# Output bias of the attention stages: one-row matmuls on TensorE, or an addition on GpSimd

## The reference

```python
# L1: cross-attention with padding mask, 16 heads
xn = layer_norm(x, g_x, b_x); kvn = layer_norm(kv, g_kv, b_kv)
... softmax(q k^T * scale) v ...
return out @ w_proj + b_proj
# L2: cross-attention, 16 heads, biases on q, k, v
return ctx @ Wo + bo
# L2 feed-forward part: first a causal self-attention without any bias
x = x + attention(layernorm(x, ln1_w), c_attn_w, c_proj_w)   # y @ c_proj_w
# L3: cross-attention, 8 heads of 64
return out @ Wout + bout
x = x + <the above>
```

## Time and profile before

| | us |
|---|---|
| median of 3 runs (lowest to highest) | 3641.53 (3633.49 to 3645.52) |
| the profiled execution, its own time | 3635.24 |
| its span, first to last instruction | 3633.5 |
| TensorE matmuls busy in the span | 2925.8 (81%) |
| VectorE busy | 2018.9 (56%) |
| ScalarE busy | 1661.6 (46%) |
| GpSimd busy | 813.2 (22%) |

### The profile page before, as it was taken

How to read it: one execution, slowest core, us unless ns; L and a number is a source line. 1 busy time by engine, 2 the same in 40 slices (tenths; PEclk the granted TensorE clock), 3 DMA queues, 4 the chain that set the end, 5 groups by cost and what they waited for, 6 DMA issues and landing times. The chain is left out here.

```text
span 3633.5 us, 71573 instructions
## 1 busy us (share of the span) xinstructions
PE 2925.8 (81%) x26488; PEld 1935.1 (53%) x26488; DVE 2018.9 (56%) x4658; ACT 1661.6 (46%) x3102; POOL 813.2 (22%) x772
## 2 busy tenths in 40 slices
PE   4888676888789999999699968996159859999932
PEld 2544353444346666666455536664158836666621
DVE  3777554777555444433477746776624335455456
ACT  2777332666534444444267635665235423333300
POOL 4332005555000000000222233430420143233000
PEclk8999796999879999999799979997579969999965
DMA  3221002111124000000111101110423323333101
GB/s 102 67 71 55 13 1 74 60 62 61 46 58 131 1 1 1 1 1 1 41 55 54 52 26 45 39 45 11 146 95 93 110 64 79 79 77 77 41 5 46
DMA packets 195045, 189.56 MB, mean 52 GB/s; under 512 B 25924, under 2 KB 173272, under 8 KB 194552
## 3 DMA queue, kind: packets, MB, share of 16 engines
q1 hardware_dynamic: 188568, 168.24, 15.0%
q0 software_dynamic: 6144, 16.79, 1.6%
HBM read 66.70 MB, written 41.42 MB: 30 GB/s over the span
## 5 line engine op out<-in xcount | busy, mean ns | idle before, releaser
L1438 DVE TENSOR_TENSOR f1H<-f1HF,f1H 128x512 bf16<-128x512 f32 x256 | 176.6, 692 | 396.6 <-ACT f1H L1283 396.6
L1216 PE MATMUL ps<-f1xT,f1w 128*128 128x512 bf16 x1536 | 378.7, 383 | 5.9 <-ACT f1H L1283 5.9
L1238 PE MATMUL ps<-f1w,f1H 128*128 128x256 bf16 x3072 | 377.8, 273 | 0.0
L1238 PEld LDWEIGHTS ps<-f1w,f1H 128*128 128x128 bf16 x3072 | 301.2, 98 | 90.0 <-issue 1.1
L1280 ACT ACTIVATE f1HF<-ps 128x512 f32<-128x512 f32 x256 | 152.8, 597 | 333.9 <-PE ps L1216 333.8
L1216 PEld LDWEIGHTS ps<-f1xT,f1w 128*128 128x128 bf16 x1536 | 148.3, 98 | 151.0 <-issue 16.9
L781 DVE TENSOR_REDUCE a0NM<-ps 128x2 f32<-128x512 f32 x256 | 166.7, 684 | 62.9 <-PE ps L480 62.5
L781 DVE TENSOR_REDUCE a1NM<-ps 128x2 f32<-128x512 f32 x256 | 166.3, 685 | 44.6 <-PE ps L480 44.1
L781 DVE TENSOR_REDUCE a2NM<-ps 128x2 f32<-128x512 f32 x256 | 165.7, 684 | 27.2 <-PE ps L480 25.9
L778 DVE TENSOR_REDUCE a3NM<-ps 128x1 f32<-128x128 f32 (+1 forms) x512 | 149.2, 348 | 43.2 <-PE ps L502 39.8
L664 ACT ACTIVATE a1PT<-ps 128x512 f32<-128x512 f32 x256 | 144.3, 595 | 51.1 <-PE ps L491 49.5
(11 more groups left out here) (563 smaller groups left out, 7085.6 us busy)
## 6 DMA issues: line engine op xcount, KB each, us to landing
a4KS<-a4KH SPq DMA_DIRECT2D x96, 128.0 KB
a4QS<-a4QH SPq DMA_DIRECT2D x96, 128.0 KB, 2.8
slots<-zeros SPq DMA_DIRECT2D x1, 9984.0 KB, 31.5
f2XS<-slots SPq DMA_DIRECT2D x39, 256.0 KB, 3.0
results<-f2XS SPq DMA_DIRECT2D x39, 256.0 KB, 2.1
f1WF<-in_f_w SPq DMA_DIRECT2D x32, 256.0 KB, 2.7
f2WF<-in_f_w SPq DMA_DIRECT2D x16, 512.0 KB, 4.8
a0KS<-a0KH SPq DMA_DIRECT2D x96, 64.0 KB
```

The source lines that it names most:

```text
L1216: m = nc.tensor.matmul(ps[:, (u * NCH + i) % 2, :], w1[:, x, kt, i * P:i * P + P], xT[:, half, y, kt, :], start=(j == 0), stop=(j == len(t ...
L1238: m = nc.tensor.matmul(out, H[:, (u * NCH + i) % HR, x, t * P:t * P + P], w2[:, y, i, :], start=first, stop=(f == YC - 1 and j == 2 and no ...
L1438: nc.vector.tensor_tensor(H[:, (u * NCH + i) % HR, 1, :], HF[:, (u * NCH + i) % 2, :], H[:, (u * NCH + i) % HR, 0, :], SUB).then_inc(S["h_ ...
```

## The change

In a1, a2 and a4 the bias is added to X itself by GpSimd, at a place of its own in the pipeline, and the two one-row matmuls per half go from all four stages. The bias row is loaded and kept in all 128 partitions (BR). The self-attention a3 is marked `plain`: it forms no bias products, loads no bias and gets no addition. VectorE's addition of the projection waits for the unit's bias addition as well.

```diff
+    biased = bool(proj) and not cfg.get("plain")
...
+        if biased:
+            put(15, "bias", "z", 0)
...
-        brow = sb("brow", [1, 2, D], BF16)
+        BR = sb("BR", [P, 2, D], F32) if biased else None
...
-                if proj:
-                    sp.dma_start(BO[0:1, 0, :], cfg["bo"]).then_inc(loaded.sem, 16)
+                if biased:
+                    sp.dma_start(BR[:, 0, :], cfg["bo"].to_broadcast([P, D])).then_inc(loaded.sem, 16)
...
+                    elif name == "bias":
+                        if u == 0:
+                            pool.wait_ge(setup.sem, base + 5)
+                        bias = BR[:, 1:2, :].to_broadcast([P, 2, D])
+                        nc.gpsimd.tensor_tensor(X[:, 2 * u:2 * u + 2, :], X[:, 2 * u:2 * u + 2, :], bias, ADD
+                                                ).then_inc(S["x_biased"].sem, 1)
...
                     if name == "weights":
-                        if proj:
+                        if biased:
                             biases()
...
-                            product3(out, [([oT[:, x, kt, t * P:t * P + P] for x in range(2)],
+                            m = product3(out, [([oT[:, x, kt, t * P:t * P + P] for x in range(2)],
                                             [wo[:, x, kt, :] for x in range(2)]) for kt in range(CK)])
-                            for x in range(2):
-                                m = nc.tensor.matmul(out, g["ones"][0:1, :], brow[0:1, x, :], start=False,
-                                                     stop=True, skip_group_check=True)
...
-                        nc.vector.tensor_tensor(BO[0:1, 1, :], ps[0:1, 1, 0:D], BO[0:1, 0, :], ADD).then_inc(setup.sem, 1)
+                        nc.vector.tensor_tensor(BR[:, 1, :], ps[:, 1, 0:D], BR[:, 0, :], ADD).then_inc(setup.sem, 1)
                         dve.wait_ge(setup.sem, base + 5)
-                        nc.vector.tensor_copy(brow[0:1, 0, :], BO[0:1, 1, :]).then_inc(setup.sem, 1)
-                        dve.wait_ge(setup.sem, base + 6)
-                        nc.vector.tensor_tensor(brow[0:1, 1, :], BO[0:1, 1, :], brow[0:1, 0, :], SUB
-                                                ).then_inc(setup.sem, 1)
-                        dve.wait_ge(setup.sem, base + 7)
...
                     elif name == "y":
                         T = Y if self_att else X
+                        if biased:
+                            dve.wait_ge(S["x_biased"].sem, S["x_biased"].at(u, 1))
...
-            att("a3", heads=16, ln=2, self=True, causal=True, proj=True)
+            att("a3", heads=16, ln=2, self=True, causal=True, proj=True, plain=True)
```

More of the change, by code:

```diff
@@ L62 @@
        "mT_ps", "m_hi", "m_lo", "st_ps", "p_ready", "pv_ps", "pv_sb", "oT_ps", "recip", "o_ready",
-       "o2T_ps", "o2_hi", "o2_lo", "y_ps", "x_done",
+       "o2T_ps", "o2_hi", "o2_lo", "y_ps", "x_done", "x_biased",
        "x_half", "x_joined"]
@@ L211, in attention @@
         VB = sb("VB", [P, CK], F32)
-        VBB = sb("VBB", [P, CK, P], F32) if proj else None
-        BO = sb("BO", [1, 2, D], F32) if proj else None
+        VBB = sb("VBB", [P, CK, P], F32) if biased else None
         CX = sb("CX", [P, 2, 2, D], F32) if own_ctx else None
@@ L244, in attention @@
         base, lbase = setup.base, loaded.base
-        all_loaded = lbase + 16 * (nw + (2 if proj else 1))
+        all_loaded = lbase + 16 * (nw + (2 if biased else 1))
         WF = PT[:].rearrange("p a n -> p (a n)").rearrange("p (w c) -> p w c", c=KT * C)
@@ L558, in _ @@
                             pe.wait_ge(S["w_lo"].sem, S["w_lo"].at(nw - 1, 1))
-                            if proj:
-                                pe.wait_ge(setup.sem, base + 7)
+                            if biased:
+                                pe.wait_ge(setup.sem, base + 5)
                         if name == "q" or self_att:
@@ L653, in _ @@
                             nc.scalar.activation(w[:, 0], f, ACT.Copy).then_inc(S["w_hi"].sem, 1)
-                        if proj:
-                            act.wait_ge(setup.sem, base + 7)
+                        if biased:
+                            act.wait_ge(setup.sem, base + 5)
                     elif name == "sst" and before is not None:
@@ L904, in attention @@
                 S[n].end(BATCH // 2 if n[-1] in "01" else BATCH)
-        setup.base += 7 if proj else 0
+        setup.base += 5 if biased else 0
         S["w_sum"].end(3)
@@ L909, in attention @@
         S["const_ready"].end(1)
-        loaded.base += 16 * (nw + (2 if proj else 1))
+        loaded.base += 16 * (nw + (2 if biased else 1))
 def signal_used(n, cfg, own_ctx, wide):
@@ L926, in signal_used @@
         return cfg.get("keep") is not None
+    if n == "x_biased":
+        return bool(proj) and not cfg.get("plain")
     if n in ("x_half", "x_joined"):
```

## The result

The changed kernel takes 3613.99 us (median of 6 runs, 3604.39 to 3616.04), the kernel before 3638.59 beside it (6 runs). The ratio is 0.9927 [0.9909, 0.9945], some 26 us less. 3608 was forecast, with 3590 to 3625 around it, so the time lies 6 us above the forecast and inside the range. The profiled execution took 3615.75 us, 19.5 less than the 3635.24 of before, where the sum had 34 less.

A forecast was written before the change was run, and what follows sets the result against it. TensorE bounds a4, SyncE's DMA queue a1 and nearly a2; a3's SyncE waits for MH. 9.8 + 8.2 + 4.2 + 0 + 10.2 + 2.3 - 1 = 33.7 less, scaled to 3608 us, range 3590 to 3625.

The forecast's parts named there:

- the sum: Whole kernel: all stage, drain, setup and clock terms together, 33.7, about 34 us less than the profiled 3635.2.
- The matmuls removed: Y block of each unit: 0.75 us goes with the one-row matmuls, at most 48 us over 64 units.
- 9.8 for thirteen: a4's full periods: TensorE is the bound, so all of 0.75 stays in 13 periods, 9.8 us.
- a3 and a2: Full periods: a3 gains 8.2 us, its SyncE waiting for MH; a2 gains 4.2, its queue nearly as late.
- a1, the step that failed: a1's full periods: SyncE's queue is the bound, so gain 0; TensorE waits 0.75 longer at each period's start.
- The clock's term: a1: longer waits may lower the granted clock after them; 1 us subtracted from the gain.
- The rival with 25 and 30 us: a1 and a2: clock at 0.88 adds 25 and 30 us of TensorE time, kernel at 3663; chance 0.05.
- Last units: Drain, the last three units of each stage: 12 x 0.75 plus 0.3 per stage, 10.2 us gained.
- The port rival: a2: bias additions beside VectorE's work cost 0.93 each, 15 us, kernel at 3623; chance 0.07.
- Setup: Stage setups: 2.3 us gained (between -1 and 6): a1 0.6, a2 0, a3 1.5, a4 0.2.
- all back: Rival, whole kernel: all of TensorE's time comes back, 55 us less, 3586; chance 0.11.

The follow-up runs named there:

- the kernels with early mask rows: a1's two mask-row transfers issued earlier, not between K and Q: on the kernel before 0.9950, 3622.41 us; on the changed kernel 0.9844, 3586.20 us.
- both, wait filled: The changed kernel with the twelve matmuls of a1's Y block issued twice, to fill TensorE's wait for the row maxima: 0.9916, 3613.29 us.
- matmuls_kept: The changed kernel with the one-row matmuls issued again on a row of zeros, bias additions kept: 1.0011 of the kernel before, 3639.37 us.
- all_but_a1: The change in a2, a3 and a4, with a1 as in the kernel before: 0.9928 of the kernel before, 3606.09 us.
- no_addition: The changed kernel without the 48 bias additions on GpSimd and VectorE's wait for them: 0.9907, 3604.75 us.
- only_a2_a3: The change in a2 and a3 only, a1 and a4 as in the kernel before: 0.9944 of the kernel before, 20 us less.
- only_a1: The change in a1 only, a2, a3 and a4 as in the kernel before: 1.0008 of the kernel before, 3637.33 us.
- mask_early_after: The changed kernel with a1's two mask-row transfers issued earlier, at the slot of the context's transposes: 0.9844, 3586.20 us.
- q_two_on_act: The changed kernel with early mask rows, and ScalarE issuing two of the six Q transfers in a0 to a3: 0.9766, 3547.22 us.
- q_four_on_act: The changed kernel with early mask rows, and ScalarE issuing four of the six Q transfers: 1.0014, 3639.21 us.

## Why the prediction was right, and where it was not

The time and its range held; several terms of the sum did not, and that the time is only 6 us off has some luck in it: the sum of the profile missed by more (34 against some 23), and the kernel before, with a median of 3641.5 in the forecast, came out at 3638.6 beside the changed one. Means over profiles with and without the change in a stage stand here (four without; three with in a1, six in the others, the kernels with early mask rows counted for a2 to a4 only).

**The matmuls removed.** 0.75 was right in a2 (2.17 to 1.42). In a4 the block lost 0.84, and the full periods lost 10.9 in twelve intervals, 0.91 each: 9.8 for thirteen was too low. Its 24 matmuls are now one run of 2.62 where two runs of twelve took 1.41 each: beside two pairs of 0.32 two ends of a run have gone, at 0.1 each.

**a3 and a2.** 8.2 was forecast for thirteen periods of a3, 5.4 came in twelve. MH now follows Q by 0.1 on the mean (Q ends 2.17 behind y, MH starts at 2.27), where the earlier trace rows showed a slack (the time between the end of the last Q issue and the start of MH's) of 0.75. The mean slack of that trace is 0.77 too, but in the four other profiles of the same code it is 0.39 to 0.48: the forecast rested on a trace in which SyncE's issues ended early, and the 5.4 / 12 = 0.45 that came is near what the others have. The reading was generous too: in that trace seven of the thirteen periods, not nine, have a slack of 0.74 or more. a2 gave 5.5 in twelve, above the 4.2 forecast. Together 10.9 against 12.4: the mechanism (SyncE's queue becomes the end of the chain) was right in both, the split was not.

**a1, the step that failed.** "Gain 0; TensorE just waits 0.75 longer" was right for the queue: MH starts 0.1 behind Q in all twelve periods and 0.8 later behind y than before (3.77 against 2.97). That the longer wait costs nothing was wrong. The periods grew by 4.1 and the setup by 2.0. What the prediction left out is that the queue waits for TensorE once per period, for K's low part: a slower TensorE behind the wait makes the queue later. That wait of SyncE is 48.8 to 50.2 us in the four profiles without the change and 51.7 to 51.9 in the three with it, 2.3 of the 4.1 us.

How much the longer wait and how much the additions cost, the runs do not divide. The table counts a long stretch at 1.2 GHz as two short ones:

| in a1 | stretches at 1.2 GHz | full periods, us |
|---|---|---|
| neither (four profiles) | 5, 5, 5, 7 | 270.5, 271.9, 271.6, 273.0 |
| additions alone | 7 | 273.3 |
| matmuls gone alone | 9 | 272.5 |
| both (three profiles) | 10, 10, 11 | 276.0, 275.1, 276.5 |
| both, wait filled | 1 | 273.6 |

Only with both is a1 clear of the scatter of the old code. One piece is plain: with the mask rows in their old place, the last of the twelve intervals takes 20.8 in all profiles with the matmuls and 22.7 to 23.0 in all without them and without a filled wait, each of these with a stretch at 1.2 GHz in it; 2 us. a2 agrees: its last interval takes 18.5 to 18.7 in five profiles of the changed stage without a stretch there, and 20.7 and 20.9 in two with one. The other eleven intervals of a1 take 249.6 to 252.1 in old code, 249.7 without the additions, and 252.1 to 253.5 with them: up to 2 us may go with the additions, but no row shows TensorE, VectorE or SyncE waiting for one, and the mask rows that GpSimd makes behind them are ready over 14 us before SyncE issues them. The clock's term, 1 us for the whole kernel, was too small: 2 us or more in a1. The rival with 25 and 30 us was far too large: a2 stayed at 0.99.

**Last units.** The stretch from the 13th to the last addition lost 1.5, 1.7 and 2.3 in a2, a3 and a4, and nothing in a1 (+0.4, in a scatter of 2.5): 5.2, with 1.9 more in the first units (from the first K product to the first addition of y). 10.2 were forecast. So of 0.75 per unit about half came back at the stages' ends; these stretches scatter by up to 2.5 us in the same code and by 5 in a4, so the shares of the stages are rough.

**GpSimd.** The addition takes 1.27, and row maxima are not slowed: their mean is 686 ns in a1, 685 before, and 690 for the twenty that overlap an addition. The mask tiles (line 438 before, 446 now) still wait for their DMA, but in 9 of 12 periods and 7.6 us in all, not in 12 and 17.2. The port rival for the steady periods of a2 is refuted, as matmuls_kept shows again (242.48). In the setup it is real: the first scaling of line 753 took 1.46 beside an addition of 1.26. The Trainium skill ("SBUF — State Buffer", Who interferes with whom) says that VectorE in a mode with two ports and GpSimd shut each other out: the one that issues first has the shared ports for its whole instruction, and the other is blocked until then. The length agrees (0.28 grown by about one addition, to 1.46). The order is not clear from the trace, since the blocked record, VectorE's, begins 0.04 ahead, and no row tells in which mode line 753 runs.

**Setup.** Forecast 2.3 gained, measured 1.9 lost: a1 2.0 longer, a2 0.4, a4 0.3, and only a3 shorter, by 0.75. (The setup is counted from the end of the stage before to the first K product.) In a1 lines 745 and 747 went, but line 753 grew from 2.20 to 3.36. That is not the addition's doing alone: in all_but_a1, where a1 is old code, line 753 took 3.39 beside other work of GpSimd. And VectorE's first use of the loads comes 14.2 to 16.0 behind the stage's start instead of 12.1 to 13.3. no_addition has it too (14.8), so it is not the addition; the load of the bias to 128 partitions, for which 0.3 was taken, is what is left. In a2, where no 2048 KB mask load is issued behind it, nothing of this shows; that the two collide is argued, not shown. In a3 TensorE's release changed as predicted:

```profile
2153.85 1.03 PE L560 MATMUL ps<-identb,a3XS 128*128 128x128 bf16 x8 [19.01 <-POOL a3XS L405]
...
2156.09 0.37 PE L479 MATMUL ps<-a3xT,a3wk 128*128 128x256 bf16 x1 [1.21 <-ACT a3xT L680]
```

K waits for ScalarE's copy behind XS and no longer for the weights. But from the stage's start XS comes 1.7 later than before (the weight work and the normalisation now run side by side), so 0.75 is left, half of the 1.5 that the sum had.

**The sum.** By stages of the profiles some 23 us were gained; by the whole times of the kernels of one or two stages 20 + 12 - 3 = 29; the pair itself has 26. The forecast's 34 was too high by about 3 in a1's periods (4.1, of which the clock's 1 was in the sum), 4 in the setups and 3 in the first and last units; a2, a3 and a4 together came out at 21.8 in the full periods against 22.2. That is why the time is within the range. The range itself was said to take in the middle of the case "all back", whose 3586 lies outside of it.

What stays open: why some periods of a1 have a stretch twice as long at 1.2 GHz. The three kernels with the whole change have two of them each, but two of the four with old code have one as well (only_a2_a3 and all_but_a1), and the kernels with one half of the change none. Open is also what the additions cost in a1, and how fast the kernel is with ScalarE issuing in a0 and a1 alone. An estimate from the stages is 3547 - 4.8 - 5.1, some 3537. That was not run.

## What to carry to other kernels

Work taken off an engine that waits for a queue anyway is not always free of cost: it lengthens the wait, TensorE may come back from it at half its clock, and if the queue later waits for TensorE, the loss comes round. So find the queue that ends last (here SyncE's DMA issues, some 0.65 us each, twelve to fourteen in a row) and shorten it first; the same removal then paid in a1 too. A DMA issue moved to another engine costs that engine the same time, and what stands behind it in its order decides whether this is a gain: in a0 it was 21 us, in a2 minus 5.

## What the runs showed of the hardware

Six transfers of 64 partitions on SyncE take 3.73 to 5.45 us to issue over all profiles, with no cause that a row shows; two on ScalarE took 1.38 in the period above. The Trainium skill ("DMA: Bandwidth & Descriptors", Issuing engines are not separate DMA queues) says that issuing on several engines saves only the issuing engine's time, usually small beside the transfer. Here the transfers of MH took 3.88 from issue to landing, and the twelve to fourteen issues in front of them some 8 to 10. This time was in the chain of a0 and a1, and of a2 and a3 once the matmuls were gone: two of six transfers moved were worth 28 us for the kernel, with 21 gained in a0 and 5 lost in a2 and in a3.

TensorE at 1.2 GHz after a wait of about 2 us is not certain. In a1 with a wait in each of twelve periods (26.5 us in all), 8 had such a stretch (9 in only_a1, with 26.5 too, and 9 in no_addition with 25.5); with 12.7 us in 8 waits, 5 had one; with waits for MH of 6.3 us in 4 (mask_early_after), 2; with none (q_two_on_act), none. MH need not be what is waited for: in a2 of q_four_on_act, where TensorE waited 38.6 us for VectorE in 39 times, up to 3.3 at once, the clock was 0.95.
